# Inverse transform of image pairs 1 to 7 in rounds inside the first steps of the two KAN layers, with one L1 accumulator instead of two

## What is computed

```python
def spectral_conv2d(x, w1, w2):
    x_ft = rfft2(x)
    out_ft[:, :, :16, :16]  = einsum('bixy,ioxy->boxy', x_ft[:, :, :16, :16], w1)
    out_ft[:, :, -16:, :16] = einsum('bixy,ioxy->boxy', x_ft[:, :, -16:, :16], w2)
    return irfft2(out_ft)
def kan_linear(x, base_w, spline_w, scaler, grid):
    return silu(x) @ base_w.T + einsum('nik,oik->no', b_splines(x, grid), spline_w * scaler[..., None])
def conv(v):
    y = spectral_conv2d(v, w1, w2) + einsum('bchw,oc->bohw', v, conv_w) + conv_b
    y = kan_linear(y, ...)          # layer 1, per pixel
    y = kan_linear(y, ...)          # layer 2, per pixel
    return gelu(y)
x = x + conv(group_norm(x))
```

## Time and profile before

| | us |
|---|---|
| median of 3 runs | 3765.86 |
| the runs | 3764.8, 3765.86, 3772.07 |
| the profiled execution | 3772.68 |
| its span, first to last instruction | 3771.0 |
| TensorE busy | 3664.2 (97%) |
| VectorE busy | 3530.6 (94%) |
| ScalarE busy | 3391.3 (90%) |
| TensorE's share of the chain that ended last | 87% |

### The profile page before, as it was taken

How to read it: one execution, slowest core, us unless ns; L and a number is a source line. 1 busy time by engine, 2 the same in 40 slices (tenths; PEclk the granted TensorE clock), 3 DMA queues, 4 the chain that set the end, 5 groups by cost and what they waited for, 6 DMA issues and landing times.

```text
span 3771.0 us, 101200 instructions
## 1 busy us (share of the span) xinstructions
PE 3664.2 (97%) x37164; PEld 1842.8 (49%) x37164; DVE 3530.6 (94%) x3917; ACT 3391.3 (90%) x3509; POOL 110.3 (3%) x131
## 2 busy tenths in 40 slices
PE   8987599999999999999999999999999999999998
PEld 4446245455455455455455455455455455455454
DVE  7764399999999999999999999999999999999997
ACT  4531399999999999999999999999999999999996
POOL 0000000000000000000000000000000000000000
PEclk9998799999999999999999999999999999999999
DMA  9998622232232232232232232332332332332321
GB/s 263 290 247 177 219 56 64 63 72 63 64 72 61 65 72 60 67 72 59 68 72 58 68 72 58 69 72 57 69 72 55 71 70 56 72 68 59 72 67 51
DMA packets 322042, 328.63 MB, mean 87 GB/s; under 512 B 86864, under 2 KB 251216, under 8 KB 319952
## 3 DMA queue, kind: packets, MB, share of 16 engines
q1 hardware_dynamic: 301152, 257.25, 25.2%
q0 software_dynamic: 18288, 66.59, 11.2%
q10 hardware_dynamic: 2560, 4.20, 0.4%
HBM read 239.88 MB, written 88.08 MB: 87 GB/s over the span
## 4 chain that ended last, share of the span: by engine, by line
PE 87%; DVE 0%; issue 0%; ACT 0%; ACTq 0%; DVEq 0%
PE l_ps L1068 82%; PE y_ps L1055 3%; PE y_ps L1047 2%; DVE cube2l L941 0%; DVE cube3r L941 0%; ACT above L983 0%; ACT offset L998 0%; ACT size L994 0%; ACT S L987 0%; ACT below L991 0%; DVE cube1r L941 0%; DVE cube1l L941 0%; DVE cube0l L941 0%; ACT L987 0%; DVE cube0r L941 0%
## 5 line engine op out<-in xcount | busy, mean ns | idle before, releaser
L998 ACT ACTIVATE offset<-size 128x1024 f32<-128x1024 f32 x1280 | 1240.4, 1044 | 8.4
L941 DVE SCALAR_TENSOR_TENSOR cube0r<-below,offset 128x1024 f32<-128x1024 f32 x256 | 312.3, 1220 | 57.1 <-ACT offset L998 56.5
L1068 PE MATMUL l_ps<-S,turned_w 64*64 64x512 f32 x2048 | 356.9, 592 | 7.8 <-issue 7.8
L1068 PE MATMUL l_ps<-cube3r,turned_w 64*64 64x512 f32 x2048 | 357.1, 589 | 0.9 <-DVE cube3r L941 0.9
L1068 PE MATMUL l_ps<-cube2r,turned_w 64*64 64x512 f32 x2048 | 356.5, 589 | 0.8 <-issue 0.8
L1068 PE MATMUL l_ps<-cube4l,turned_w 64*64 64x512 f32 x2048 | 357.1, 589 | 0.1
L1068 PE MATMUL l_ps<-cube3l,turned_w 64*64 64x512 f32 x2048 | 357.1, 589 | 0.1
L1068 PE MATMUL l_ps<-cube4r,turned_w 64*64 64x512 f32 x2048 | 357.1, 589 | 0.1
L1068 PE MATMUL l_ps<-bowl,turned_w 64*64 64x512 f32 x2048 | 357.1, 589 | 0.0
L1068 PE MATMUL l_ps<-inner_cube,turned_w 64*64 64x512 f32 x2048 | 357.1, 589 | 0.0
L1068 PE MATMUL l_ps<-cube0r,turned_w 64*64 64x512 f32 x2048 | 356.4, 591 | 0.6 <-DVE cube0r L941 0.6
(11 more groups left out here) (122 smaller groups left out, 6852.2 us busy)
## 6 DMA issues: line engine op xcount, KB each, us to landing
big<-in_x_dram SPq DMA_DIRECT2D x128, 512.0 KB, 7.0
x_ring<-in_x_dram SPq DMA_DIRECT2D x256, 256.0 KB, 4.1
out_dram<-act_out SPq DMA_DIRECT2D x128, 512.0 KB, 2.7
act_out<-in_x_dram POOLq DMA_DIRECT2D x127, 512.0 KB, 6.8
rows_scratch<-rows SPq DMA_DIRECT2D x16, 1024.0 KB, 7.0
rows_t<-rows_scratch SPq DMA_DIRECT2D x512, 32.0 KB, 5.5
big<-in_spec_w_r_dram SPq DMA_DIRECT2D x16, 512.0 KB, 11.4
big<-in_spec_w_i_dram SPq DMA_DIRECT2D x16, 512.0 KB, 11.4
```

Source lines behind the costliest of these rows:

```text
L941: nc.vector.scalar_tensor_tensor(out=cube[q][side][:], in0=distance[layer][:], scalar=EDGE - KNOTS[q], in1=offset[layer][q][:], op0=ALU.mi ...
L998: nc.scalar.activation(offset[layer][q][:], size[layer][:], ACT.Square, bias=-KNOTS[q]).then_inc(offset_ready[layer], 1)
L1068: ins = nc.tensor.matmul(dst[cols, r * MM:(r + 1) * MM], kan_w[layer][rows_, f, :], src[rows_, n * MM:(n + 1) * MM], start=(f == 0), stop= ...
```

## The change

The block `inverse_rows` goes. Its loads, matmuls, copies and stores move into `second_half`:

- the four rounds of pair 0 stand ahead of everything, in four PSUM tensors that are free then; SP stores of pair 0 first only the 16 image lines that tiles 0 and 1 need (`FIRST_ROWS`, two transfers of 128 KB), loads them back, and stores the other 112 lines after that;
- the 28 rounds of pairs 1 to 7 stand two to a step in steps 2 to 15, each after the sixth product of a layer;
- their copies stand on ScalarE at the start of the following part of a step (ahead of `take`, and so ahead of `gelu`), on VectorE after the cubes of the fourth knot;
- all rounds share one PSUM tensor, `inv_ps`; a round waits for both copies of the round before it. To make room, layer 1 has one accumulator, `l1_ps`; only tile 1 uses `inv_ps` instead. So layer 1 of tile t, from tile 3 on, waits for `S` of layer 2 of tile t-1;
- SP stores a pair's rows (2 MB) and loads a later pair's modes in steps 5 to 17, behind the output store of that step;
- steps 2 to 17 are written out, the loop starts at step 18.

```diff
@@ SP in second_half
+            load_spec(0)
+            for u in range(2):
+                sp.dma_start(inv_h_sb[u * K:(u + 1) * K], t["inv_h"]).then_inc(inv_h_loaded, 16)
+            load_x(sp, t, place(0))
+            load_spec(1)
+            sp.wait_ge(x_loaded, 32)
+            load_x(sp, t, place(1))
+            for u in range(2):
+                sp.wait_ge(rows_kept[u], BANKS)
+                store_rows(0, u, 0, FIRST_ROWS, first_rows_stored)
+            load_spec(2)
+            sp.wait_ge(first_rows_stored, 32)
+            load_rows(sp, t, place(0))
+            for u in range(2):
+                store_rows(0, u, FIRST_ROWS, H, rows_stored[0][u])
+            sp.wait_ge(rows_loaded, 64)
+            load_rows(sp, t, place(1))
...
+            for j in range(2, 2 * PAIRS + AHEAD + 1):
...
+                pair = (j - AHEAD - 1) // 2
+                if j % 2 == 1 and 1 <= pair < PAIRS:
+                    for u in range(2):
+                        sp.wait_ge(rows_kept[u], BANKS * (pair + 1))
+                        store_rows(pair, u, 0, H, rows_stored[pair % 2][u])
+                    if pair + 2 < PAIRS:
+                        load_spec(pair + 2)
@@ helpers
-        y_ps, l2_ps = ps("y_ps"), ps("l2_ps")
-        l1_ps = [ps("l1_ps0"), ps("l1_ps1")]
+        y_ps, l1_ps, l2_ps = ps("y_ps"), ps("l1_ps"), ps("l2_ps")
+        inv_ps = ps("inv_ps")
+        def l1_of(like):
+            return inv_ps if like == 1 else l1_ps
+        def round_of(i, like, pos):
+            n = BANKS + 2 * (i - 2) + pos if isinstance(i, int) and i >= 2 else None
+            return n if n is not None and n < BANKS * PAIRS else None
+        def keep_round(eng, n, u, copy):
+            pair, k = n // BANKS, n % BANKS
+            if k == 0 and pair >= 2:
+                eng.wait_ge(rows_stored[pair % 2][u], 16 * (pair // 2))
+            eng.wait_ge(rows_done[u], n + 1)
+            copy(rows_out[pair % 2][u][:, k * MM:(k + 1) * MM], inv_bank(n, u)).then_inc(rows_kept[u], 1)
-        LOOP0, LOOP1 = 2, TILES - 4
+        LOOP0, LOOP1 = 2 + 2 * PAIRS, TILES - 4
@@ VectorE step
+                        if q == 3:
+                            n = round_of(i, like, pos - 1) if pos else round_of(i - 1, like - 1, 1)
+                            if n is not None:
+                                keep_round(dve, n, 1, nc.vector.tensor_copy)
@@ ScalarE step
+                    n = round_of(i, like, pos - 1) if pos else round_of(i - 1, like - 1, 1)
+                    if n is not None:
+                        keep_round(act, n, 0, copy)
                     after = following(i, like, layer)
@@ TensorE
+            def inverse_round(n):
+                pair, k = n // BANKS, n % BANKS
+                if k == 0:
+                    pe.wait_ge(spec_loaded[pair % 2], 32 * (pair // 2 + 1))
+                part, cols = k // (BANKS // 2), k % (BANKS // 2) * MM
+                for u in range(2):
+                    if pair > 0:
+                        pe.wait_ge(rows_kept[u], n)
+                    own = slice(u * K, (u + 1) * K)
+                    nc.tensor.matmul(inv_bank(n, u), inv_h_sb[own, part, :], spec[pair % 2][own, cols:cols + MM],
+                                     start=True, stop=True, tile_position=(u * K, 0)).then_inc(rows_done[u], 1)
...
-                        pe.wait_ge(S_ready[1], tile - 1)
+                        pe.wait_ge(S_ready[1], tile if like_ > 2 else tile - 1)
...
+                        n = round_of(i, like, pos)
+                        if q == 1 and n is not None:
+                            inverse_round(n)
```

More of the change, by code:

```diff
@@ L172, in load_tile, with load_rows @@
           .then_inc(t["x_loaded"], 16)
+def load_rows(sp, t, where):
+    pair, k, slot, par = where
+    rows_in = t["rows_dram"].rearrange("(p i) (t n h) (q o) -> p i t n q h o", i=2, n=2, h=HH, o=C)
+    for n in range(2):
         for i in range(2):
@@ L680, in _ @@
                             ins.then_inc(normed_ready, 1)
[L683 to L764, removed]
-                            nc.tensor.matmul(ps[u][k][:], inv_h_sb[own, part, :], spec[p][own, cols:cols + MM],
-                                             start=True, stop=True, tile_position=(u * K, 0)).then_inc(rows_done[u], 1)
[L768 to L772, removed]
-            with eng.Fori(0, PAIRS // 2) as pair2:
-                for p in range(2):
-                    eng.wait_ge(rows_stored[p][u], 16 * (pair2 + 1))
-                    for k in range(BANKS):
-                        eng.wait_ge(rows_done[u], 2 * BANKS * pair2 + (BANKS * p + k + 1))
-                        copy(rows[p][u][:, k * MM:(k + 1) * MM], ps[u][k][:]).then_inc(rows_kept[u], 1)
-        @block.scalar
-        def _(act):
-            keep(act, 0, lambda dst, src_: nc.scalar.activation(dst, src_, ACT.Copy))
-        @block.vector
-        def _(dve):
-            keep(dve, 1, nc.vector.tensor_copy)
@@ L891, in _ @@
                 sp.wait_ge(y_done, j)
                 load_tile(sp, t, place(j))
-            with sp.Fori(AHEAD, TILES) as j:
+                if j >= AHEAD:
+                    sp.wait_ge(x_added, 16 * (j - (AHEAD - 1)))
+                    store(place(j - AHEAD))
+                pair = (j - AHEAD - 1) // 2
+                if j % 2 == 1 and 1 <= pair < PAIRS:
+                    for u in range(2):
+                        sp.wait_ge(rows_kept[u], BANKS * (pair + 1))
+                        store_rows(pair, u, 0, H, rows_stored[pair % 2][u])
+                    if pair + 2 < PAIRS:
+                        load_spec(pair + 2)
@@ L894, in _ @@
+            for p in range(2):
+                for u in range(2):
+                    sp.wait_ge(rows_stored[p][u], 16 * (PAIRS // 2))
+            with sp.Fori(2 * PAIRS + AHEAD + 1, TILES) as j:
                 loaded, stored = place(j), place(j - AHEAD)
@@ L953, in step @@
             def step(i, like):
-                for layer, tile, like_ in work(i, like):
+                for pos, (layer, tile, like_) in enumerate(work(i, like)):
                     for q in range(NK):
@@ L963, in _ @@
             nc.vector.tensor_scalar(l1_shift[:], kan_b[0][:], EDGE, None, ALU.add).then_inc(shift_ready, 1)
+            for n in range(BANKS):
+                keep_round(dve, n, 1, nc.vector.tensor_copy)
             steps(dve, step)
@@ L1095, in step @@
                     product(dst, layer, F_CUBE, inner_cube).then_inc(used[layer], 1)
+            pe.wait_ge(inv_h_loaded, 32)
+            for n in range(BANKS):
+                inverse_round(n)
             y(0, 0, -2)
```

41 lines of the change are left out of this document (34 added, 7 removed).

## The result

The changed kernel takes 3747.66 us (median of 5 runs, 3745.88 to 3748.2), the kernel before, run beside it, 3768.13 (5 runs, 3764.8 to 3772.07). The ratio is 0.9945, with a 95% interval of 0.9932 to 0.9959: 20.5 us or 0.55% faster. The forecast was 26.8 us, and 3739. The profiled execution took 3745.88 us (span 3743.7), against 3772.68 before, exactly the 26.8 of the forecast. That agreement is luck: two errors of 7 to 8 us, with opposite signs, nearly cancel in this pair of executions, and only one of them belongs to the change.

What follows compares the result with a forecast made beforehand. TensorE was taken to bound the second half, transfers the stage ahead of it. Terms of -60.6, +32.8, +0.2, 0 and +0.8 gave -26.8 us, from 3765.9 to 3739 us; 8-in-10 range 3727 to 3750.

Steps and rivals of the forecast that it cites:

- The bound: Second half, from 496 us: TensorE's own work sets the 25.77 us step; ScalarE and VectorE have some 0.3 us of room.
- Term 1: Start of the second half: `y` of tile 0 starts at 378.5 us instead of 439.10, -60.6 us.
- The rival of the late start: Before `y` of tile 0: small stores and row loads wait behind modes and x, 6.2 us less gain, 3745; chance 0.08.
- Term 2: Steps 2 to 15: 28 rounds add their full length on TensorE, 1.17 us each with shape changes, +32.8 us.
- the rival without a price for the shape: Rounds on TensorE: changing matmul shape costs nothing, so the 28 rounds add 24.1 us, total 3730; chance 0.18.
- Term 3: Round copies on ScalarE and VectorE: TensorE stays the bound, only the first copy is close, +0.2 us.
- The first close copy: VectorE's copy in step 2, ending at 541.45 as TensorE reaches the second round at 541.4: wait of 0 to 0.5 us, once.
- Term 4: Single layer 1 accumulator: layer 1 waits for `S` of the tile before, with 0.4 us of room at the tightest, 0 us.
- The rival that was slower than before: Single accumulator: ScalarE's late reads make TensorE wait 0.35 us in each of 112 steps, 39 us, 3778; chance 0.03.
- Term 5: Steps with rounds: moved transfers cost 0, sixteen more steps of straight code one TensorE stall, +0.8 us.
- The rival of a stop at each piece of code: TensorE's straight code: a stall twice a step in 14 steps, 22 us, 3760; chance 0.06.

Runs made afterwards that it cites:

- Quarters: Changed kernel with each round as four 64x64 matmuls instead of two 64x128: 3736.69 us, run again 3739.02 us.
- the kernel with earlier modes: Changed kernel with four 64x64 matmuls a round, TensorE's steps 2 to 15 as a loop, modes loaded after TensorE's round, not its copies: 3731.37 us.
- the one edit alone: Kernel before with one layer 1 accumulator, the other for tile 1 alone, and the change's waits: 3768.74 us, ratio 1.0003.
- the loop: Changed kernel with TensorE's steps 2 to 15 as a loop and modes loaded earlier, rounds whole, bursts in place: 3740.64 us.

## Why the prediction was right or wrong

**The bound** held. Steps without rounds are 25.76 or 25.77 us, TensorE waits for no engine in the steps, and each round adds its whole length.

**Term 1 was right**, -60.6 forecast, -60.4 in the trace, and 60.4 to 62.1 with the other traces (18.1 to 19.8 us instead of 80.16). Two of its links were off by as much in opposite directions: the 128 KB stores landed after 3.3 us and not 2.7, the row loads after 2.2 and not 2.8. The first round waited for the table `inv_h_sb` and not for the modes. I had the table land 1.5 us ahead of them; it landed last, at the time that I had given the modes. Tile 1 came 7.59 us later, as covered as I said. The rival of the late start fell.

**Term 2 was right in its mechanism, and a little small**: 1.22 us a round and not 1.17. The forward transform's alternation between 128x64 and 128x128 costs 0.31 us both ways, this one 0.36. Quarters took that off and left 0.86, so the rival without a price for the shape is refuted; it described a kernel that could have been written.

**Term 3 held.** The first close copy cost 0.3 to 0.4 us (a step of 28.63 and one of 28.52, against 28.21) where I had 0 to 0.5. In the kernel with earlier modes the wait is in the records by name:

```profile
480.13 1.09 PE L1102 MATMUL inv_ps<-spec,inv_h_sb 64*64 64x512 f32 x8 [0.26 <-DVE rows L770]
```

ScalarE, with its two copies, had the room that was forecast: its waits at `gelu` in steps with rounds went up to 1.8 us (3.2 behind a stop).

**Term 4 held**: no cost, shown by the one edit alone. The rival that was slower than before fell with it.

**Term 5 is the step that failed.** I put 0.8 us on more straight code and nothing on the transfers, each judged by itself: the tail's straight code runs without a stop, and 2.5 MB of transfers wait for nobody. Their meeting was not in the sum. Bursts alone do no harm (the loop), straight code alone little (none in these steps with all rounds, 2.8 us without them); both together cost 7.9 us in one trace, 4.4 in the other (482.29 against 477.89), 5 to 7 by the medians. The rival of a stop at each piece of code was the right mechanism with the wrong rule for when it strikes: three stops beside 35 pieces of code, and each behind a burst.

**The base.** The forecast stood on a median of three runs, 3765.9; with five it was 3768.1. Of the 8.7 us between forecast and result, 2.3 are that, some 5 to 7 the stops, 1.4 the rounds. The profile after agreed to 0.1 us with the forecast only because its first half was 7.4 us shorter by chance, and its end, behind the steps with rounds, 2.2.

## What to carry to other kernels

When bulk transfers move beside an engine that is the bound and whose code is written out, look at the pairing, not at each: a piece of code that must be fetched in or behind a burst can stop the engine (here 3 of 35), and a loop avoided it. Thinner bursts left smaller stops in the one trace. Insert foreign work into a stream of matmuls in the tile shape of the stream, even as more instructions. And before two single profiles are subtracted, compare a part that the edit doesn't touch; here it moved by up to 9.0 us.

## What the hardware showed that I had not expected

- **A stop of TensorE can be paid twice.** After idling 2.93 us it went on at a granted clock of 0.66 over 4.1 us, after 4.07 us at 0.50 over 6 us, which is the lower of its two levels, 1.2 instead of 2.4 GHz. The 4.07 us cost 7.2, the 2.93 us 5.6. The length of the idle time alone does not decide: in the trace of quarters alone a stop with 1.98 us idle was followed by 0.64 over 4.7 us (step 3.8 us longer), one with 2.39 us by the full clock (2.7 longer). Behind the two shorter stops of the changed kernel (steps longer by 1.2 and 1.1 us) the clock, the last column but two of the busy time by stretch, stayed full:

```profile
585.80:592.00 6.20, 6.20 (x50) 2.30 (x54) 5.00 (x6) 6.20 (x8) 0.00 (x0) 1.00 0.03 6
...
818.90:825.00 6.10, 6.01 (x52) 2.05 (x55) 5.10 (x5) 6.08 (x8) 0.00 (x0) 1.00 0.00 0
```
- **A piece of code can come late behind data.** With the rows' traffic the pieces of 16 KB that TensorE stopped for came 3.2 to 5.4 us later in their step than without it, and it went on 2.3 to 2.7 us after each. That they waited behind the burst's packets, and at which point of their way, no view shows. The Trainium skill, page "Runtime: NRT & Kernel Launch", section "Instruction fetch mechanics", calls the cost of crossing 16 KB of code mostly hidden. That holds here for most pieces and not for the stops: written-out steps lost 2.8 us against the loop with none of the rows' traffic, 4.4 to 7.9 us with it. The section also says that a branch to code outside the part already fetched breaks the prefetch, and gives this as a reason to unroll. Here the turns of the loop cost nothing, 27.48 us a step to the hundredth; whether their target had to be fetched no view shows.
